# Pixel additions leave GpSimd's queue as their products are done, and SyncE branches ahead of its last wait

## The chip, the core and the metric

The kernel runs on one core of one Trainium2 chip. Its time is device microseconds (us) of one execution on that core; three executions give the median and the spread. Five engines work side by side and meet only at semaphores: TensorE (PE, with its weight loads as PEld), VectorE (DVE), ScalarE (ACT), GpSimd (POOL) and SyncE (SP), which here only issues transfers. Each engine takes its instructions strictly in the order in which they stand in its queue.

## The reference

The input x is 8 images of 24 channels and 64x64 pixels, float32. Two residual stages are computed, both with a normalisation over the 24 channels of a pixel:

```python
x = x + _L0_conv_ref(_ln_c(x))
t = _to_tokens(x)
t = t + _L0_ffn_ref(_ln_t(t), L0_ffn_W1, L0_ffn_b1, L0_ffn_W2, L0_ffn_b2)
x = _from_tokens(t, x)
```

`_L0_conv_ref` multiplies its input by V / (V + 1e-6), a share per pixel that depends on how uneven the channel mean of the normalised input is. That mean is zero but for rounding, so the map is flat and the share is a constant table, unless a check made at run time says otherwise. `_L0_ffn_ref` is a two-layer network (24 to 96, bias, relu, 96 to 24, bias) on values rounded to 8-bit floats (5 exponent bits, 2 mantissa bits), with sums rounded to 16-bit floats.

## The kernel before

The 32768 pixels stand as 8 groups (n = 0 to 7) of 128 partitions x 32 pixels, each with 24 channels: 128x768 float32, 384 KB. For statistics the groups are taken in four units of 1, 1, 2 and 4 groups (u = 0 to 3). Everything stays in on-chip memory between the 9 loads at the start and the 9 stores.

For one group the steps are, with the function that issues each:

- VectorE `centre(n)` (L806): pixels minus the channel mean. The means come from `reduce_pixels` for groups 0 and 1, and else from sums made on TensorE, which `take_sums` copies (L797, L795).
- ScalarE `square(n)`, TensorE `sum_squares(n)` (L607), VectorE `take_var(u)` (L813), ScalarE `first_std(u)`, VectorE `inverse_std(u)` and `conv_gain(s, u)` (three short instructions): the factor by which a centred pixel is multiplied in the first stage.
- the product centred x gain into `result`: `conv(s, n)`, on GpSimd (L372) for groups 0, 1, 2, 4, 5, 6 and on VectorE (L844) for groups 3 and 7.
- `add_pixels(s, n)` (L360): a transfer issued by GpSimd that adds the loaded pixels to `result` in memory.
- ScalarE `second_std`, VectorE `second_inverse`, `second_norm`, and `quantise(s, n)` (L863): the second normalisation, rounded to 8 bits. TensorE `turn(s, n)` (L625) turns it, ScalarE `copy_turned` (L447) copies it.
- the network's first layer in three tiles t = 0, 1, 2: TensorE `first_layer(s, n, t)` (L640), ScalarE `round_hidden(s, n, t)` (L456), VectorE `bias_relu(s, n, t)` (L875), then `quantise_hidden` (L884) for tiles 0 and 1 together and for tile 2.
- the second layer: TensorE `second_layer(s, n)` (L662), ScalarE `round_ffn` (L466), VectorE `second_bias` (L892).
- the last addition: for groups 0 to 4 `add_ffn_by_dma(s, n)` (L366), again a transfer issued by GpSimd; for groups 5 to 7 `add_ffn` on VectorE (L903). Then `store(s, n)` (L327) on SyncE; the last half of group 7 is stored by ScalarE (L473).

`unevenness()`, `find_peak()` and `flag()` make the run-time check; every engine loads its flag (L290) and branches over a second, general pass that is not run on this input. `keep_busy(s, n)` (L675) is three matmuls on zeros whose result nobody reads.

Nothing schedules this work at run time or build time: the order in each queue is written out by hand, as the list of calls in a function `first_groups` of each engine. In the GpSimd list a few waits stand that no data needs, such as `pool.wait_ge(s.hidden_act, 9)`: they set the moment at which a product begins. Waits that data does need stand inside the functions.

## Time and profile before

| what | value |
|---|---|
| three executions | 67.58, 67.95 and 67.13 us, median 67.58 |
| profiled execution | 67.71 us, of which the traced span is 65.8 us |
| VectorE busy | 54.9 us, 83% of the span |
| TensorE busy | 52.0 us, 79% |
| ScalarE busy | 44.1 us, 67% |
| GpSimd busy | 23.9 us, 36% |
| transfers | 12.07 MB in 4475 packets |

The profile comes from one execution. "Busy" counts compute instructions; on GpSimd the issue of an adding transfer is counted too. A duration includes the end of an instruction that overlaps the start of the next one on the same engine, so what an instruction costs its queue is the distance between two starts. Start times are microseconds from the start of the span; the 1.9 us between 67.71 and the span lie outside the trace.

### The profile page before, as it was taken

The page shows a single profiled execution, that of the slowest core. Times are in us where ns is not written, and L with a number is a line of the kernel's source. Part 1 is how long each engine was busy: PE and PEld are TensorE (multiplying, and loading weights), DVE is VectorE, ACT ScalarE, POOL GpSimd, SP SyncE. Part 2 cuts the span into 40 slices and gives each one's busy share as a digit, 9 for nine tenths or more (in the row PEclk, how much of TensorE's full clock was granted, in tenths as well). Part 3 has the DMA queues.
Part 4 walks back from the last instruction along what each step waited for, and adds up shares of the span by engine and source line. Part 5 has one row for each costly group of instructions (what it writes and reads, how often), then busy time and mean ns, then how long its engine had stood idle before and what let it go on. Part 6 is the DMA issues. An engine that isn't in the chain of part 4 may idle for free.

```text
span 65.8 us, 1346 instructions
## 1 busy us (share of the span) xinstructions
PE 52.0 (79%) x471; PEld 36.5 (55%) x475; DVE 54.9 (83%) x113; ACT 44.1 (67%) x67; POOL 23.9 (36%) x25
## 2 busy tenths in 40 slices
PE   2999999999999999959759978979996988460000
PEld 0334999999998999826128335518262627150000
DVE  2059957899799999799999999999999999999300
ACT  5304352287749999279999999999999994450000
POOL 2000001964830000389387989962350580000000
PEclk9999999999999999999999999999999999999655
DMA  0999999009339000001995996999999399999651
GB/s 0 240 420 350 407 405 393 17 10 181 58 60 179 0 0 0 0 0 33 198 187 103 202 228 132 187 312 233 263 286 218 73 304 291 274 284 342 251 177 36
DMA packets 4475, 12.07 MB, mean 183 GB/s; under 512 B 496, under 2 KB 752, under 8 KB 4464
## 3 DMA queue, kind: packets, MB, share of 16 engines
q0 software_dynamic: 1872, 5.11, 39.1%
q1 hardware_dynamic: 2448, 6.62, 27.0%
q10 hardware_dynamic: 144, 0.20, 0.9%
q8 instruction: 6, 0.10, 0.8%
q14 instruction: 5, 0.04, 0.2%
HBM read 3.67 MB, written 3.15 MB: 104 GB/s over the span
## 4 chain that ended last, share of the span: by engine, by line
PE 49%; DVE 16%; ACT 13%; issue 12%; DVEq 2%; ACTq 0%
PE ps_ffn L607 12%; ACT hidden_rounded L456 10%; PE ps_ffn L589 8%; PE ps_ffn L764 8%; PE ps_hidden L640 6%; DVE hidden_q L884 5%; PE ps_ffn L662 5%; PE ps_ffn L579 4%; PE ps_hidden L607 4%; DVE ffn_out L892 3%; DVE hidden_act L875 2%; ACT packed_t L447 2%; DVE result L903 2%; DVE packed L863 1%; PE ps_turned L625 1%
## 5 line engine op out<-in xcount | busy, mean ns | idle before, releaser
L456 ACT ACTIVATE hidden_rounded<-ps_hidden 128x1024 f16<-128x1024 f32 x24 | 23.8, 1031 | 0.0
L372 POOL TENSOR_TENSOR result<-centred,gain 128x768 f32<-128x768 f32 x6 | 11.2, 1866 | 21.4 <-DVE scaled_var L837 10.4
L640 PE MATMUL ps_hidden<-packed_t,w1q 96*128 96x512 fp8e5 x48 | 14.0, 380 | 1.5 <-ACT packed_t L447 0.8
L875 DVE TENSOR_SCALAR hidden_act<-hidden_rounded,b1q 128x1024 f16<-128x1024 f16 x24 | 11.5, 478 | 0.0
L425 ACT ACTIVATE squares<-centred 128x768 f32<-128x768 f32 (+1 forms) x9 | 6.8, 769 | 4.6 <-DVE centred L806 4.6
L662 PEld LDWEIGHTS ps_ffn<-w2q,hidden_q 128*128 128x128 fp8e5 x168 | 7.6, 98 | 2.9 <-DVE hidden_q L884 2.4
L360 POOL DMA_DIRECT2D result<-loaded x8 | 8.4, 1103 | 1.8 <-POOL result L372 1.5
L662 PE MATMUL ps_ffn<-w2q,hidden_q 128*128 128x96 fp8e5 x168 | 8.3, 206 | 0.7 <-DVE hidden_q L884 0.7
L884 DVE TENSOR_SCALAR hidden_q<-hidden_act 128x2048 uint16<-128x2048 uint16 (+1 forms) x16 | 8.8, 549 | 0.1
L607 PEld LDWEIGHTS ps_ffn<-squares,loaded 128*128 128x128 f32 x72 | 8.6, 192 | 0.4
L607 PE MATMUL ps_ffn<-squares,loaded 128*128 128x128 f32 x72 | 8.7, 275 | 0.0
L806 DVE SCALAR_TENSOR_TENSOR centred<-ps_values,loaded 128x768 f32<-128x768 f32 (+1 forms) x9 | 7.5, 863 | 0.1
L863 DVE TENSOR_TENSOR packed<-centred,ps_values 128x768 fp8e5<-128x768 f32 x8 | 7.4, 946 | 0.0
L366 POOL DMA_DIRECT2D result<-ffn_out x5 | 4.6, 919 | 6.4 <-DVE ffn_out L892 5.9
L640 PEld LDWEIGHTS ps_hidden<-packed_t,w1q 96*128 96x128 fp8e5 x48 | 3.5, 98 | 5.4 <-ACT hidden_rounded L456 2.3
L466 ACT ACTIVATE ffn_rounded<-ps_ffn 128x768 f16<-128x768 f32 x7 | 5.7, 816 | 1.1 <-DVE ffn_out L892 1.0
L764 PE MATMUL ps_ffn<-warm 128*128 128x512 bf16 x12 | 5.3, 629 | 1.2 <-DVE warm L1175 1.2
L589 PE MATMUL ps_ffn<-loaded 128*128 128x128 f32 x48 | 5.7, 276 | 0.0
L589 PEld LDWEIGHTS ps_ffn<-loaded 128*128 128x128 f32 x48 | 5.5, 192 | 0.0
L786 DVE TENSOR_REDUCE ps_values<-loaded 128x32 f32<-128x768 f32 x2 | 3.0, 1482 | 2.8 <-DMA loaded<-in_load 2.8
L447 ACT ACTIVATE packed_t<-ps_turned 96x512 bf16<-96x512 bf16 x8 | 4.8, 599 | 0.5 <-PE ps_turned L625 0.4
L892 DVE TENSOR_TENSOR ffn_out<-ffn_rounded,b2q 128x768 f16<-128x768 f16 (+1 forms) x9 | 5.0, 562 | 0.0
(54 smaller groups left out, 54.5 us busy)
## 6 DMA issues: line engine op xcount, KB each, us to landing
result<-loaded POOLq DMA_DIRECT2D x8, 384.0 KB, 4.6
out<-result SPq DMA_DIRECT2D x7, 384.0 KB, 3.5
loaded<-in_load SPq DMA_DIRECT2D x6, 384.0 KB, 6.1
result<-ffn_out POOLq DMA_DIRECT2D x5, 384.0 KB, 5.2
loaded<-in_load SPq DMA_DIRECT2D x2, 448.0 KB, 4.1
loaded<-in_load SPq DMA_DIRECT2D x1, 385.5 KB, 7.8
out<-result SPq DMA_DIRECT2D x1, 192.0 KB, 2.5
out<-result ACTq DMA_DIRECT2D x1, 192.0 KB, 4.0
```

The source lines that it names most:

```text
L360: pool.dma_start(result[:, n], pixels[n], accum_op=ALU.add).then_inc(s.residual[n], 16)
L372: nc.gpsimd.tensor_tensor(result[:, n], centred[:, n], group_values(gain, n), ALU.mult).then_inc(s.conv_pool, 1)
L456: nc.scalar.activation(hidden_rounded[:, i % HIDDEN_BUFS], ps_hidden[:, i % 2], ACT.Copy).then_inc(s.hidden_rounded, 1)
L589: last = nc.tensor.matmul(ps_late_channels, ident, late_pixels[:, :, c, :], start=(c == 0), stop=(c == C - 1))
L607: last = nc.tensor.matmul(ps_square[u][:, n - UNIT_START[u]], ident, squares[:, n, c * GPIX:(c + CB) * GPIX], start=(c == 0), stop=(c == C ...
L640: last = nc.tensor.matmul(ps_hidden[:, i % 2, b * BANK:(b + 1) * BANK], w1q[:, t * P:(t + 1) * P], packed_t[:, n % 2].bitcast(E5M2)[:, b:: ...
L662: last = nc.tensor.matmul(ffn_banks(n)[:, half, at * CQ:(at + 1) * CQ], hidden_q[:, n % 2, t, col * P:(col + 1) * P].bitcast(E5M2)[:, 0::2 ...
L764: nc.tensor.matmul(ps_ffn[:, i % 2], warm[:, 0:P], warm[:], start=True, stop=True)
L806: nc.vector.scalar_tensor_tensor(centred[:, n, lo:hi, :], group_values(channel_sums, n)[:, lo:hi, :], -1.0 / C, pixels[n][:, lo:hi, :], AL ...
L863: nc.vector.tensor_tensor(packed[:, n % 2].rearrange("p j (c q) b -> p j c b q", q=Q), centred[:, n].rearrange("p c (j b q) -> p j c b q", ...
L875: nc.vector.tensor_scalar(hidden_act[:, n % 2, t], hidden_rounded[:, (n * TILES + t) % HIDDEN_BUFS], b1q[:, t:t + 1], 0.0, ALU.add, ALU.ma ...
L884: nc.vector.tensor_scalar(hidden_q[:, n % 2, lo:hi], hidden_act[:, n % 2, lo:hi].bitcast(U16), 1.0 / 256, None, ALU.mult).then_inc(s.hidde ...
```

## The change

No instruction is added or dropped, but for one jump on SyncE. On GpSimd each pixel addition now follows the product it needs: group 3's addition comes ahead of group 2's product, group 7's ahead of the second transfers of groups 1 to 4, and the first product waits for a later event. The waits that set when products begin are others. On SyncE group 3 is stored ahead of group 2, and the wait for all stores stands behind the branch. On VectorE, ScalarE and TensorE the lists of calls are put in another order.

```diff
@@ SyncE
                 store(s, 0)
                 store(s, 1)
+                store(s, 3)
                 store(s, 2)
-                store(s, 3)
                 store(s, 4)
...
             uneven_map = is_uneven(sp)
-
-            sp.wait_ge(flat_pass.stored, 16 * (NG + 1))
             with sp.If(uneven_map):
+
+                sp.wait_ge(flat_pass.stored, 16 * (NG + 1))
...
+            sp.wait_ge(flat_pass.stored, 16 * (NG + 1))
@@ GpSimd
-                pool.wait_ge(s.scaled_var, 1)
+                pool.wait_ge(s.norm2, 2)
                 conv(s, 0)
                 add_pixels(s, 0)
-                pool.wait_ge(s.norm2, 2)
+                pool.wait_ge(centred_vector, 6)
                 conv(s, 1)
                 add_pixels(s, 1)
-                pool.wait_ge(s.hidden_act, 4)
+                add_pixels(s, 3)
+                pool.wait_ge(s.hidden_q, 2)
                 conv(s, 2)
                 add_pixels(s, 2)
-                add_pixels(s, 3)
-                pool.wait_ge(s.hidden_act, 6)
+                add_ffn_by_dma(s, 0)
+                pool.wait_ge(s.hidden_act, 5)
                 conv(s, 4)
                 add_pixels(s, 4)
-                add_ffn_by_dma(s, 0)
-                pool.wait_ge(s.hidden_act, 9)
+                pool.wait_ge(s.norm2, 4)
                 conv(s, 5)
                 add_pixels(s, 5)
+                add_pixels(s, 7)
                 add_ffn_by_dma(s, 1)
-                pool.wait_ge(s.hidden_act, 11)
+                pool.wait_ge(s.hidden_act, 12)
                 conv(s, 6)
...
                 add_ffn_by_dma(s, 4)
-                add_pixels(s, 7)
@@ TensorE
-                second_layer(s, 1)
@@ VectorE
+                conv(s, 7)
...
-                conv(s, 7)
```

How the queues stand now, first GpSimd's, from group 2's product on. Before (L372 is a product, L360 a pixel addition, L366 the addition of the network's output; the wait in brackets tells the group of the last two kinds):

```order
L372 TENSOR_TENSOR result<-centred,gain 128x768 [waits centred_vector,gain0,hidden_act0]
L360 DMA result<-loaded 128x768 [waits conv_pool0]
L360 DMA result<-loaded 128x768 [waits conv_vector0]
L372 TENSOR_TENSOR result<-centred,gain 128x768 [waits centred_vector,gain0,hidden_act0]
L360 DMA result<-loaded 128x768 [waits conv_pool0]
L366 DMA result<-ffn_out 128x768 [waits ffn_out0,residual0_0]
L372 TENSOR_TENSOR result<-centred,gain 128x768 [waits centred_vector,gain0,hidden_act0]
L360 DMA result<-loaded 128x768 [waits conv_pool0]
L366 DMA result<-ffn_out 128x768 [waits ffn_out0,residual0_1]
```

And in the changed kernel, from group 3's pixel addition on (every line number is one higher):

```order
L361 DMA result<-loaded 128x768 [waits conv_vector0]
L373 TENSOR_TENSOR result<-centred,gain 128x768 [waits centred_vector,gain0,hidden_q0]
L361 DMA result<-loaded 128x768 [waits conv_pool0]
L367 DMA result<-ffn_out 128x768 [waits ffn_out0,residual0_0]
L373 TENSOR_TENSOR result<-centred,gain 128x768 [waits centred_vector,gain0,hidden_act0]
L361 DMA result<-loaded 128x768 [waits conv_pool0]
L373 TENSOR_TENSOR result<-centred,gain 128x768 [waits centred_vector,gain0,norm2_0]
L361 DMA result<-loaded 128x768 [waits conv_pool0]
L361 DMA result<-loaded 128x768 [waits conv_vector0]
L367 DMA result<-ffn_out 128x768 [waits ffn_out0,residual0_1]
```

Group 5's product now waits for `second_norm` of the last unit and no longer stands behind group 0's second transfer; both additions that wait for VectorE's products (conv_vector0) have moved ahead.

The second place is VectorE, from the second `second_inverse` of the last unit to the middle of group 2's hidden tiles. Before:

```order
L849 RECIPROCAL inv_std<-std 128x128
L875 TENSOR_SCALAR hidden_act<-hidden_rounded,b1q 128x1024
L884 TENSOR_SCALAR hidden_q<-hidden_act 128x1024
L892 TENSOR_TENSOR ffn_out<-ffn_rounded,b2q 128x8x24x4
L875 TENSOR_SCALAR hidden_act<-hidden_rounded,b1q 128x1024
L854 SCALAR_TENSOR_TENSOR ps_values<-gain,inv_std 128x128
L875 TENSOR_SCALAR hidden_act<-hidden_rounded,b1q 128x1024
L863 TENSOR_TENSOR packed<-centred,ps_values 128x96x2x4 x2
L892 TENSOR_TENSOR ffn_out<-ffn_rounded,b2q 128x8x24x4
```

Now:

```order
L850 RECIPROCAL inv_std<-std 128x128
L876 TENSOR_SCALAR hidden_act<-hidden_rounded,b1q 128x1024
L885 TENSOR_SCALAR hidden_q<-hidden_act 128x2048
L855 SCALAR_TENSOR_TENSOR ps_values<-gain,inv_std 128x128
L864 TENSOR_TENSOR packed<-centred,ps_values 128x96x2x4 x2
L876 TENSOR_SCALAR hidden_act<-hidden_rounded,b1q 128x1024
L885 TENSOR_SCALAR hidden_q<-hidden_act 128x1024
L876 TENSOR_SCALAR hidden_act<-hidden_rounded,b1q 128x1024
L845 TENSOR_TENSOR result<-centred,gain 128x768
```

The two `quantise` calls (L863, now L864) come sooner behind `second_norm`, `second_bias` of group 0 has gone to an earlier place and that of group 1 to a later one, and group 7's product stands here in place of 10 us further on.

The third place is TensorE, from `keep_busy(s, 1)` on. Before:

```order
L675 MATMUL ps_ffn<-warm 128x512 x3
L625 MATMUL ps_turned<-ident_bf,packed 96x128 x4
L640 MATMUL ps_hidden<-packed_t,w1q 128x512 x4
L662 MATMUL ps_ffn<-w2q,hidden_q 128x96 x24
L640 MATMUL ps_hidden<-packed_t,w1q 128x512 x4
```

Now:

```order
L676 MATMUL ps_ffn<-warm 128x512 x3
L641 MATMUL ps_hidden<-packed_t,w1q 128x512 x4
L626 MATMUL ps_turned<-ident_bf,packed 96x128 x4
L641 MATMUL ps_hidden<-packed_t,w1q 128x512 x6
L626 MATMUL ps_turned<-ident_bf,packed 96x128 x4
L641 MATMUL ps_hidden<-packed_t,w1q 128x512 x2
L626 MATMUL ps_turned<-ident_bf,packed 96x128 x4
L663 MATMUL ps_ffn<-w2q,hidden_q 128x96 x24
```

Group 1's second layer (x24) has moved behind two more tiles of the first layer and two more turns.

## Rows read from the trace of the kernel before

**Rows 1.** The page: busy us; DMA in 40 slices; the second layer (24 matmuls a group).

```profile
PE 52.0 (79%) x471; PEld 36.5 (55%) x475; DVE 54.9 (83%) x113; ACT 44.1 (67%) x67; POOL 23.9 (36%) x25
...
DMA  0999999009339000001995996999999399999651
...
L662 PE MATMUL ps_ffn<-w2q,hidden_q 128*128 128x96 fp8e5 x168 | 8.3, 206 | 0.7 <-DVE hidden_q L884 0.7
```

**Rows 2.** Timeline of VectorE: start us, us, what, xcount, [idle before <-releaser].

```profile
27.72 0.69 DVE L813 TENSOR_REDUCE square_sums<-ps_ffn 128x128 f32<-128x512 f32 x1 [0.44 <-PE ps_ffn L607]
...
33.98 0.54 DVE L875 TENSOR_SCALAR hidden_act<-hidden_rounded,b1q 128x1024 f16<-128x1024 f16 x1
...
34.78 0.55 DVE L892 TENSOR_TENSOR ffn_out<-ffn_rounded,b2q 128x768 f16<-128x768 f16 x1
35.25 0.48 DVE L875 TENSOR_SCALAR hidden_act<-hidden_rounded,b1q 128x1024 f16<-128x1024 f16 x1
35.64 0.29 DVE L854 SCALAR_TENSOR_TENSOR ps_values<-gain,inv_std 128x128 f32<-128x128 f32 x1
...
36.24 1.81 DVE L863 TENSOR_TENSOR packed<-centred,ps_values 128x768 fp8e5<-128x768 f32 x2
37.97 1.04 DVE L892 TENSOR_TENSOR ffn_out<-ffn_rounded,b2q 128x768 f16<-128x768 f16 x1
...
42.38 0.58 DVE L875 TENSOR_SCALAR hidden_act<-hidden_rounded,b1q 128x1024 f16<-128x1024 f16 x1
```

**Rows 3.** Timeline of GpSimd: three of its six products.

```profile
32.43 1.80 POOL L372 TENSOR_TENSOR result<-centred,gain 128x768 f32<-128x768 f32 x1 [1.01 <-DVE hidden_act L875]
...
36.46 2.13 POOL L372 TENSOR_TENSOR result<-centred,gain 128x768 f32<-128x768 f32 x1
...
40.82 1.85 POOL L372 TENSOR_TENSOR result<-centred,gain 128x768 f32<-128x768 f32 x1
```

**Rows 4.** Timeline of ScalarE.

```profile
28.45 0.40 ACT L432 ACTIVATE std<-square_sums,eps_c 128x128 f32<-128x128 f32 x1 [1.76 <-DVE square_sums L813]
...
31.19 0.81 ACT L466 ACTIVATE ffn_rounded<-ps_ffn 128x768 f16<-128x768 f32 x1
...
32.17 1.93 ACT L456 ACTIVATE hidden_rounded<-ps_hidden 128x1024 f16<-128x1024 f32 x2
33.98 0.61 ACT L447 ACTIVATE packed_t<-ps_turned 96x512 bf16<-96x512 bf16 x1
34.46 1.96 ACT L456 ACTIVATE hidden_rounded<-ps_hidden 128x1024 f16<-128x1024 f32 x2
...
53.08 1.94 ACT L456 ACTIVATE hidden_rounded<-ps_hidden 128x1024 f16<-128x1024 f32 x2
```

**Rows 5.** Timeline of VectorE, the end.

```profile
56.45 0.48 DVE L875 TENSOR_SCALAR hidden_act<-hidden_rounded,b1q 128x1024 f16<-128x1024 f16 x1
...
60.43 1.03 DVE L903 TENSOR_TENSOR result<-result,ffn_out 128x384 f32<-128x384 f32 x2
```

**Rows 6.** Timeline of TensorE: the last sums of squares.

```profile
24.84 2.84 PE L607 MATMUL ps_ffn<-squares,loaded 128*128 128x128 f32 x24
```

**Rows 7.** Stretches: busy us (instructions) of PE, PEld, DVE, ACT, POOL; granted PE clock; DMA share; GB/s.

```profile
32.60:34.60 2.00, 1.13 (x8) 0.36 (x6) 2.00 (x4) 2.00 (x4) 1.70 (x2) 1.00 1.04 189
...
38.00:50.00 12.00, 10.45 (x110) 5.74 (x110) 12.00 (x25) 12.00 (x17) 7.24 (x7) 1.00 0.97 232
...
62.00:65.80 3.80, 0.00 (x0) 0.00 (x0) 0.00 (x0) 0.00 (x0) 0.00 (x0) 0.50 0.38 130
```

**Rows 8.** By line: the stores' landings (L327, then L473), SyncE's branch, VectorE's last instruction.

```profile
DMA to landing us min/median/max: 2.4/3.4/5.1
...
DMA to landing us min/median/max: 4.0/4.0/4.0
...
L345 SPq COMPARE_BRANCH  x1: 45/45/45, 65.5 to 65.5; - x1
...
L151 DVEq DRAIN  x1: 62/62/62, 64.8 to 64.8; - x1
```

More of the change, by code:

```diff
@@ L512, in first_groups @@
                 first_std(2)
+                square(6)
+                copy_turned(s, 1)
                 round_hidden(s, 0, 1)
[L514 to L515 removed]
                 second_std(s, 2)
+                square(7)
                 round_hidden(s, 0, 2)
[L518 removed]
+                first_std(3)
                 round_hidden(s, 1, 0)
[L520 removed]
+                round_ffn(s, 0)
                 round_hidden(s, 1, 1)
@@ L523, in first_groups @@
                 round_hidden(s, 1, 2)
-                round_ffn(s, 0)
                 second_std(s, 3)
@@ L721, in first_groups @@
                 second_layer(s, 0)
+                first_layer(s, 1, 1)
+                first_layer(s, 1, 2)
+                turn(s, 2)
+                keep_busy(s, 1)
                 first_layer(s, 2, 0)
                 first_layer(s, 2, 1)
-                keep_busy(s, 1)
                 turn(s, 3)
@@ L1079, in first_groups @@
                 centre(1)
+                take_sums(0)
+                centre(2)
                 take_var(0)
+                centre(3)
                 inverse_std(0)
+                take_var(1)
                 conv_gain(s, 0)
-                take_sums(0)
+                inverse_std(1)
+                conv_gain(s, 1)
                 second_inverse(s, 0)
-                take_var(1)
-                centre(2)
-                inverse_std(1)
                 second_norm(s, 0)
-                conv_gain(s, 1)
                 quantise(s, 0)
@@ L1092, in first_groups @@
                 second_norm(s, 1)
-                centre(3)
                 quantise(s, 1)
@@ L1108, in first_groups @@
                 bias_relu(s, 0, 2)
+                second_norm(s, 2)
                 quantise_hidden(s, 0, 2, 3)
-                second_norm(s, 2)
-                bias_relu(s, 1, 0)
                 take_var(3)
@@ L1114, in first_groups @@
                 inverse_std(3)
+                bias_relu(s, 1, 0)
+                second_bias(s, 0)
+                conv_gain(s, 3)
                 bias_relu(s, 1, 1)
-                conv_gain(s, 3)
-                quantise_hidden(s, 1, 0, 2)
-                bias_relu(s, 1, 2)
                 quantise(s, 3)
                 second_inverse(s, 3)
+                bias_relu(s, 1, 2)
+                quantise_hidden(s, 1, 0, 2)
+                second_norm(s, 3)
+                quantise(s, 4)
+                quantise(s, 5)
                 bias_relu(s, 2, 0)
                 quantise_hidden(s, 1, 2, 3)
-                second_bias(s, 0)
                 bias_relu(s, 2, 1)
-                second_norm(s, 3)
+                conv(s, 7)
                 bias_relu(s, 2, 2)
-                quantise(s, 4)
-                quantise(s, 5)
-                second_bias(s, 1)
                 quantise_hidden(s, 2, 0, 2)
                 bias_relu(s, 3, 0)
+                second_bias(s, 1)
+                bias_relu(s, 3, 1)
                 quantise_hidden(s, 2, 2, 3)
-                bias_relu(s, 3, 1)
+                bias_relu(s, 3, 2)
                 quantise(s, 6)
                 quantise(s, 7)
-                bias_relu(s, 3, 2)
+                bias_relu(s, 4, 0)
                 quantise_hidden(s, 3, 0, 2)
-                bias_relu(s, 4, 0)
+                bias_relu(s, 4, 1)
                 quantise_hidden(s, 3, 2, 3)
-                bias_relu(s, 4, 1)
                 second_bias(s, 2)
@@ L1147, in first_groups @@
                 second_bias(s, 3)
+                unevenness()
                 quantise_hidden(s, 5, 0, 2)
                 bias_relu(s, 5, 2)
-                conv(s, 7)
+                second_bias(s, 4)
+                quantise_hidden(s, 5, 2, 3)
                 bias_relu(s, 6, 0)
-                quantise_hidden(s, 5, 2, 3)
                 bias_relu(s, 6, 1)
-                second_bias(s, 4)
-                unevenness()
+                flag()
                 bias_relu(s, 6, 2)
@@ L1159, in first_groups @@
                 quantise_hidden(s, 6, 2, 3)
-                flag()
+                second_bias(s, 5)
                 bias_relu(s, 7, 1)
-                second_bias(s, 5)
                 quantise_hidden(s, 7, 0, 2)
```

63 lines of the change are left out of this document (28 added, 35 removed).

## The prediction

> **What bounds the kernel now.** I read the page first [rows 1]: VectorE is the busiest engine at 54.9 us, and TensorE's 52.0 us hold three-matmul fillers that nobody waits for. The DMA row has a hole between 22 and 30 us and stands at 9 almost without a break from 31 to 61 us. Then the timelines. From 17.7 us to its last addition at 61.46 us [rows 5] VectorE has one wait of any size, 0.44 us at 27.72 [rows 2], for the last sums of squares. ScalarE waits 1.76 us for the same event [rows 4] and is busy for all of the 12 us from 38 to 50 [rows 7]. So in the middle both queues are full, and the question for any order is which of them is late at the end. In the profile it is VectorE: ScalarE has rounded its last hidden tile at 55.02 (53.08 + 1.94) [rows 4], VectorE takes it at 56.45 [rows 5]. That is a slack of 1.43 us for ScalarE. Behind 56.45 the end is fixed work: additions up to 61.46, the last store 4.0 us to landing, the branch on SyncE at 65.5, the end at 65.8 [rows 5, 8].
>
> Since no compute instruction is added or dropped, the sum of VectorE's steps stays. The time can move only by what VectorE loses between them: stalls behind GpSimd, waits for others, and the tail.
>
> **Steps used below**, each a distance between two starts: a bias step 0.39 to 0.40 (35.25 to 35.64), a `quantise` 0.87 (36.24 to 37.97 for two) [rows 2]; on ScalarE a hidden tile 0.91 (32.17 to 33.98 for two), a turned copy 0.48 (33.98 to 34.46), `round_ffn` 0.7 (its 0.81 less the 0.1 by which such instructions overlap) [rows 4].
>
> **Stalls behind GpSimd's products.** Three VectorE instructions are longer than their like: the bias step at 33.98 has 0.54 instead of 0.48, `second_bias` at 37.97 has 1.04 instead of 0.55, the bias step at 42.38 has 0.58 instead of 0.48 [rows 2]: 0.06 + 0.49 + 0.10 = 0.65 us. Each began while a product ran, and ended 0.3 to 0.4 us after it: the products end at 34.23, 38.59 and 42.67 [rows 3]; the VectorE instructions at 34.52, 39.01 and 42.96. `quantise` beside a product keeps its 0.9 us [rows 2]. So a product costs what pokes out beyond the pair of `quantise` calls that it is put under. Before, group 5's product stands behind group 0's second transfer in GpSimd's queue, begins 0.2 us late and pokes out over a `second_bias`. Now its wait is `second_norm` of the last unit, whose next instructions are two `quantise`: product 1.81 plus some 0.1 of signalling against 2 x 0.87, so it reaches 0.1 to 0.2 into the bias step behind it. Group 6's now waits for the bias step just ahead of two `quantise`, as it did before in effect: 0.10. Group 4's begins ahead of `quantise` and `second_inverse`, as before: 0.06. Sum now 0.10 + 0.10 + 0.06 = 0.26, so **-0.39 us**. Bounds: -0.65 if none pokes out, 0 if the 0.49 comes back at another instruction. Groups 0, 1 and 2 now run under `quantise`, `centre` and `take_var`, which no row shows slowed: 0. Group 7's product on VectorE changes place, not cost.
>
> **The last sums of squares.** On TensorE `first_layer(1, 0)` moves behind them, so they end 0.43 us sooner than 27.68 (24.84 + 2.84) [rows 6], and VectorE's `take_var` starts at 27.28 instead of 27.72. But the bias step that before filled the gap ahead of it (0.40) now comes after: **-0.04 us**. ScalarE had that hidden tile done before its 1.76 us of waiting; now it has 0.91 more to do behind it and the start is 0.44 earlier, so it runs about 0.4 us later than before from here on, which eats into its slack of 1.43.
>
> **New waits of VectorE.** I walked the new order through with the steps above. From 27.28: `take_var` 0.6 (its 0.69 less the overlap [rows 2]), `quantise` 0.87, `inverse_std` as much, bias 0.40, and `second_bias(0)` could begin at 30.01. Its input: TensorE's second layer begins when the variance is taken (28.02) and takes 1.2 (24 of 168 matmuls with 8.3 us, [rows 1]); `round_ffn` begins at 29.3 and ends at 30.1, so a wait of 0.06. `second_inverse(3)` meets its input within 0.02. In the middle VectorE carries group 7's product (0.87) ahead of group 1's `second_bias`, and ScalarE stays ahead. At 47.65 `second_bias(3)` waits for `round_ffn(3)`, whose chain ends near 47.8: 0.17. Near the end the run-time check (1.7 us) now stands ahead of `quantise_hidden` of group 5, so `round_ffn(5)` waits about 0.7 us on ScalarE and the last hidden tile is ready near 55.8 instead of 55.02; VectorE needs it near 56.2. That holds, with 0.4 to 0.5 us left of 1.43. Sum **+0.25 us**; bounds 0 and +1.2 (each of the three double, and the last tile 0.7 late).
>
> **Branch and stores.** SyncE's branch takes 45 ns at 65.5, its engine ends 0.1 later [rows 8]. Now the branch runs while the last store is under way, but a jump stands behind the wait: **-0.05 us**, bounds -0.1 and 0 for this part alone. The pixel addition of group 7, before issued at 52 us into full DMA engines, goes out near 39 us, that of group 3 near 24 us into the hole. No compute instruction waits for either. Group 3's store ahead of group 2's makes the latter wait for a landing near 53.5 us, but five more stores follow anyway. Left is the last store: 4.0 us to landing, where the fastest of the other eight took 2.4 [rows 8]. With less queued it could land earlier, but not for more than 0.7 us of gain, because VectorE's own last instruction stands at 64.8 [rows 8]. Value taken **0**, since the stores of the last three groups and their spacing stay; bounds -0.7 and +0.5.
>
> **Sum.** -0.39 - 0.04 + 0.25 - 0.05 = -0.23 us. Against the profiled execution 67.71 that is 67.48; this one lies 0.13 above the median of 67.58, so the forecast is **67.35 us**.
>
> **Rivals.**
>
> *The tail gets shorter too.* For it: the last store's 4.0 us against 2.4, and 0.9 to 1.0 of DMA share up to 61 us [rows 1, 8], of which one adding transfer of 384 KB is taken away. Against it: stores of groups 2 and 3 move later. Price: the 0.7 above, 66.65 us. Chance 0.25.
>
> *TensorE's clock falls (slower).* Between `keep_busy(1)` and the second layer of group 1, some 31 to 37.7 us, TensorE now has only six first-layer tiles and three turns, each behind a ScalarE step, with gaps up to 0.85 us. The granted clock held 1.00 over 1.13 us of work in 2.00 and shows 0.50, the lower level of 1.2 GHz, after nothing was run [rows 7]. Decides: whether the new light stretch is lighter than the one that held. At the lower level 10.45 us of work in 12.00 [rows 7] is 20.9; if 4 us of that stretch run so, the delay is 4 x (2 x 0.87 - 1) = 3.0, less the slack of 1.43: +1.5 us, 68.85. Chance 0.1.
>
> *VectorE starves.* The waits at +1.2 instead of +0.25, with the stalls saved: 68.3 us. For it: ScalarE keeps less than 0.5 of its slack. Chance 0.1.
>
> *The branch doesn't save but costs.* On VectorE the branch is done near 61.6 and the next instruction stands at 64.8 [rows 8], 3.2 us later. If SyncE's new jump behind the last wait did likewise, the end would come 1 to 3.2 us later, 68.4 to 70.5. Against it: SyncE's queue is short, and its branch before let it go on within 0.1 us [rows 8]. The Trainium skill (Runtime: NRT & Kernel Launch, Instruction fetch mechanics) says that a taken branch whose target isn't in the current two-page window must first fetch the page. By that page VectorE's 3.2 us is such a fetch, which this trace agrees with, and SyncE's jump costs nothing if its few instructions share the window; the time would be 67.35 in one case and 68.4 or more in the other. Chance 0.05.
>
> **How the numbers follow.** The forecast's own case has 0.5. A measurement here tells about 1% from no change (the three runs spread over 0.8 us): below 66.90 is faster, above 68.26 slower. Faster: the tail's 0.25 and a fifth of the forecast's case, 0.35. Slower: 0.1 + 0.05 + 0.05 of the starved case's 0.1, 0.2. Same: 0.45. The range takes in the tail rival with the full -0.65 of the stalls (66.65 - 0.26, 66.4) and reaches up to the starved case and the short end of the dear branch, 68.5.
>
> **What the profile after would show.** Right: no `second_bias` above 0.6 us between 30 and 45 us; `take_var` of the last unit near 27.3; ScalarE's last hidden tile within 0.5 us of VectorE's use; VectorE's last addition ending near 61.2; granted clock 1.00 up to the last matmul. Wrong: idle rows of VectorE that name ScalarE and add up to over 0.5 us, a DRAIN of SyncE well after the last landing, or a last store that lands in under 3 or over 4.5 us; the last alone moves the time by more than all my terms.

## The result and the profile after

| | before | after |
|---|---|---|
| executions, us | 67.58, 67.95, 67.13, 67.20 | 69.30, 69.43, 70.17, 69.38 |
| median, us | 67.39 | 69.41 |
| profiled execution, us (span) | 67.71 (65.8) | 69.30 (67.4) |

The changed kernel is slower: ratio 1.034, 95% interval 1.028 to 1.041. The forecast was 67.35 us with a range up to 68.5. Ratios here and below leave out executions that took over 1.5% longer than the fastest of the same kernel, and so can differ from the quotient of the medians.

The page of the changed kernel, beside [rows 1]: busy us, then the granted TensorE clock and the DMA share in 40 slices of 1.7 us.

```profile
PE 53.9 (80%) x471; PEld 37.6 (56%) x475; DVE 55.1 (82%) x113; ACT 44.2 (66%) x67; POOL 23.3 (35%) x25
...
PEclk9999999999999999999985556999999999999555
DMA  0899999000029481908675999955799819986570
```

VectorE does the same work, 55.1 us against 54.9. What stands out is the clock row: four slices of 5 and 6 in the middle of the work. The profile dates them: the granted clock was 0.50, the lower level of 1.2 GHz, from 34.9 to 41.7 us. Before, it held 1.00 until TensorE had run out of work. The DMA row has thinned from 44 us on, and the time has not followed. In stretches (columns as in [rows 7]) the new order looks so:

```profile
32.00:34.00 2.00, 1.60 (x8) 0.50 (x8) 2.00 (x4) 2.00 (x4) 2.00 (x2) 1.00 0.75 156
34.00:36.00 2.00, 1.03 (x5) 0.25 (x4) 1.97 (x5) 2.00 (x4) 1.67 (x3) 0.72 0.46 106
36.00:38.00 2.00, 2.00 (x9) 0.91 (x8) 2.00 (x4) 1.47 (x2) 1.70 (x2) 0.50 0.93 275
38.00:40.00 2.00, 2.00 (x17) 1.29 (x16) 2.00 (x5) 2.00 (x3) 0.92 (x2) 0.50 1.00 182
40.00:42.00 2.00, 2.00 (x20) 1.49 (x18) 1.00 (x2) 1.09 (x2) 0.75 (x1) 0.57 0.96 174
```

From 36 us TensorE is busy without a gap at the lower clock, and in the last stretch VectorE is idle for half of the time (1.00 of 2.00). The timeline of TensorE names the work (start us, us, what, idle before):

```profile
34.20 0.60 PE L641 MATMUL ps_hidden<-packed_t,w1q 96*128 96x512 fp8e5 x2 [0.18 <-ACT hidden_rounded L457]
...
35.59 1.95 PE L641 MATMUL ps_hidden<-packed_t,w1q 96*128 96x512 fp8e5 x4 [0.79 <-ACT packed_t L448]
...
37.76 1.06 PE L641 MATMUL ps_hidden<-packed_t,w1q 96*128 96x512 fp8e5 x2
...
39.16 2.13 PE L663 MATMUL ps_ffn<-w2q,hidden_q 128*128 128x96 fp8e5 x24
...
43.59 1.19 PE L663 MATMUL ps_ffn<-w2q,hidden_q 128*128 128x96 fp8e5 x24
```

Two first-layer matmuls took 0.60 us at 34.20 and 1.06 at 37.76. Group 1's second layer took 2.13 us, and the same 24 matmuls for the next group, with the clock at 1.00 again, 1.19. The delay is passed on to ScalarE's `round_ffn` and from there to VectorE. ScalarE first, then VectorE:

```profile
41.33 0.81 ACT L467 ACTIVATE ffn_rounded<-ps_ffn 128x768 f16<-128x768 f32 x1 [0.91 <-PE ps_ffn L663]
```

```profile
27.67 0.69 DVE L814 TENSOR_REDUCE square_sums<-ps_ffn 128x128 f32<-128x512 f32 x1 [0.58 <-PE ps_ffn L608]
...
30.75 0.56 DVE L893 TENSOR_TENSOR ffn_out<-ffn_rounded,b2q 128x768 f16<-128x768 f16 x1 [0.35 <-ACT ffn_rounded L467]
...
42.24 0.56 DVE L893 TENSOR_TENSOR ffn_out<-ffn_rounded,b2q 128x768 f16<-128x768 f16 x1 [1.24 <-ACT ffn_rounded L467]
...
45.57 0.75 DVE L876 TENSOR_SCALAR hidden_act<-hidden_rounded,b1q 128x1024 f16<-128x1024 f16 x1
...
62.66 1.03 DVE L904 TENSOR_TENSOR result<-result,ffn_out 128x384 f32<-128x384 f32 x2
```

At 42.24 `second_bias(1)` comes after 1.24 us of idleness, nearly three times the largest wait before [rows 2]. The stalled `second_bias` at 37.97 of [rows 2] is gone, but a bias step at 45.57 now has 0.75 instead of 0.48. GpSimd says why:

```profile
43.34 0.85 POOL L367 DMA_DIRECT2D result<-ffn_out  x1 [2.59 <-DVE ffn_out L893]
44.06 1.97 POOL L373 TENSOR_TENSOR result<-centred,gain 128x768 f32<-128x768 f32 x1
```

Group 1's second transfer stands ahead of group 6's product in the queue, and waited 2.59 us for the late `second_bias(1)`. The product started behind it, at 44.06, and ended at 46.03, 0.29 us before the bias step did. This loss isn't the clock's: with the clock at 1.00, in `after_fill_again` below, the transfer waits 1.25 us and the bias step behind the product still has 0.75.

The span is 1.6 us longer. Cut at VectorE's copy of the last unit's channel sums (17.73 us before, 17.98 after), its last `take_var` and the end of its last addition, that is:

| part | before | after | difference |
|---|---|---|---|
| start, to the copy of the sums | 17.73 | 17.98 | +0.25 |
| copy to `take_var` (27.72, 27.67) | 9.99 | 9.69 | -0.30 |
| `take_var` to VectorE's last addition (61.46, 63.69) | 33.74 | 36.02 | +2.28 |
| tail | 4.34 | 3.71 | -0.63 |

The start's +0.25 goes with a late load: TensorE waited 1.30 us for one in this execution and had no such wait in the one before. In the third part I compared the distances from each VectorE start to the next, step by step: `second_bias(1)` +1.33; the bias step that now follows the variance +0.40; `second_bias(0)` +0.35 (0.35 idle); `second_norm` +0.12; a `quantise_hidden` that uses the bias step directly ahead of it +0.12; stalls beside GpSimd's work 0.53 instead of 0.65, so -0.12. These make 2.20 of the 2.28.

### The profile page after: what moved, and what is told of

Same layout as the page of the kernel before. It is cut to its first block, busy times and chain, and to the rows that moved or that the text cites. A ratio compares the mean times of both kernels' runs of the same rounds, so it can differ in the third digit from the quotient of the medians.

```text
span 67.4 us, 1347 instructions
## 1 busy us (share of the span) xinstructions
PE 53.9 (80%) x471; PEld 37.6 (56%) x475; DVE 55.1 (82%) x113; ACT 44.2 (66%) x67; POOL 23.3 (35%) x25
## 4 chain that ended last, share of the span: by engine, by line
PE 47%; DVE 20%; issue 8%; ACT 8%; DMA 7%; DVEq 2%; SPq 1%; ACTq 0%
PE ps_ffn L608 12%; PE ps_ffn L663 8%; PE ps_ffn L590 8%; DMA loaded<-in_load 7%; PE ps_hidden L641 7%; DVE hidden_act L876 5%; ACT ffn_rounded L467 4%; PE ps_ffn L580 4%; PE ps_hidden L608 4%; DVE ffn_out L893 4%; DVE hidden_q L885 3%; DVE packed L864 2%; ACT hidden_rounded L457 2%; PE ps_turned L626 2%; DVE result L904 2%
## 5 line engine op out<-in xcount | busy, mean ns | idle before, releaser
L641 PE MATMUL ps_hidden<-packed_t,w1q 96*128 96x512 fp8e5 x48 | 15.4, 418 | 2.0 <-ACT packed_t L448 1.3
L663 PEld LDWEIGHTS ps_ffn<-w2q,hidden_q 128*128 128x128 fp8e5 x168 | 8.4, 104 | 3.4 <-DVE hidden_q L885 2.1
L663 PE MATMUL ps_ffn<-w2q,hidden_q 128*128 128x96 fp8e5 x168 | 9.3, 217 | 0.9 <-DVE square_sums L814 0.6
L361 POOL DMA_DIRECT2D result<-loaded x8 | 7.6, 956 | 5.4 <-DVE result L845 3.6
L864 DVE TENSOR_TENSOR packed<-centred,ps_values 128x768 fp8e5<-128x768 f32 x8 | 7.4, 948 | 0.1
L893 DVE TENSOR_TENSOR ffn_out<-ffn_rounded,b2q 128x768 f16<-128x768 f16 (+1 forms) x9 | 4.5, 509 | 1.6 <-ACT ffn_rounded L467 1.6
L765 PE MATMUL ps_ffn<-warm 128*128 128x512 bf16 x12 | 4.2, 520 | 1.2 <-DVE warm L1176 1.2
```

Of the source, the lines that this page charges most:

```text
L361: pool.dma_start(result[:, n], pixels[n], accum_op=ALU.add).then_inc(s.residual[n], 16)
L641: last = nc.tensor.matmul(ps_hidden[:, i % 2, b * BANK:(b + 1) * BANK], w1q[:, t * P:(t + 1) * P], packed_t[:, n % 2].bitcast(E5M2)[:, b:: ...
L663: last = nc.tensor.matmul(ffn_banks(n)[:, half, at * CQ:(at + 1) * CQ], hidden_q[:, n % 2, t, col * P:(col + 1) * P].bitcast(E5M2)[:, 0::2 ...
L864: nc.vector.tensor_tensor(packed[:, n % 2].rearrange("p j (c q) b -> p j c b q", q=Q), centred[:, n].rearrange("p c (j b q) -> p j c b q", ...
```

## The experiments

Each label begins with the kernel that was edited. Every experiment was timed beside `before` on the same chip, whose median is given with it. "Stretch" is the third part of the table above, `take_var` to the end of the last addition: it holds every edit and neither the loads nor the last store, whose durations differ from execution to execution. Its values are 33.74 us for `before` and 36.02 for `after`.

### Is it the clock? `after_fill`, `after_again`, `after_fill_again`

Nine matmuls on zeros, whose result nobody reads, go between the first-layer tiles of the changed kernel, so that TensorE has work where it waited for ScalarE. `fill(k)` is k matmuls of the kind in `keep_busy`.

```diff
                 keep_busy(s, 1)
+                fill(2)
                 first_layer(s, 2, 0)
+                fill(1)
                 first_layer(s, 2, 1)
                 turn(s, 3)
+                fill(2)
                 first_layer(s, 2, 2)
+                fill(3)
                 first_layer(s, 3, 0)
+                fill(1)
                 first_layer(s, 3, 1)
```

> The changed kernel with nine extra filler matmuls (128x512, results unread) on TensorE between keep_busy(1) and group 1's second layer: 2 before and 1 after first_layer(2,0), 2 after turn(3), 3 after first_layer(2,2), 1 after first_layer(3,0). Clock theory: granted clock 1.00 from the start to the last matmul, VectorE's wait for round_ffn(1) falls from 1.24 us to under 0.4, the time to 67.3 to 67.9 us. Rival, the order itself makes group 1's second layer late: the clock holds but VectorE still waits about 1 us there and the time stays at 68.8 us or more.

Measured: median 69.03 us, above the 67.3 to 67.9 expected, beside a before median of 68.04, ratio 1.017 (1.006 to 1.029). The profiled execution had late loads (TensorE waited 2.39 us for one, and took 70.62 us in all), but its stretch is 34.72, the granted clock is 1.00 throughout the middle and `second_bias(1)` doesn't wait. The interval was wide, so I ran the same kernel again beside an unchanged `after`.

> The changed kernel once more, beside the two with fillers on the same chip. Clock theory: granted clock 0.50 for some 6.8 us from about 35 us, VectorE's wait for round_ffn(1) near 1.2 us, time 2 to 3% above the kernel before. If the fall of the clock was an accident of one execution: this profile shows 1.00 there and a ratio near that of the filled kernel.

> The changed kernel with nine extra fillers ahead of group 1's second layer, once more. Clock theory: 1.00 throughout the middle, 1.0 to 1.5 us faster than the changed kernel on the same chip, so 0.5 to 1.2% above the kernel before. Rival, the order alone: within 0.3 us of the changed kernel.

Measured: `after_again` 69.51 us, ratio 1.027 (1.021 to 1.033), stretch 35.47; `after_fill_again` 67.99, ratio 1.008 (1.002 to 1.014), stretch 34.72; before median 67.58. By the medians the fillers give back 1.52 us; in the two profiled executions the stretch shows 0.75 of it, and the rest lies in the start and the tail. Stretches of `after_again`, then of `after_fill_again`:

```profile
34.80:38.20 3.40, 2.22 (x12) 0.69 (x10) 3.37 (x7) 3.39 (x5) 2.80 (x3) 1.00 0.63 182
38.30:41.70 3.40, 3.31 (x32) 2.77 (x32) 3.03 (x6) 2.63 (x3) 1.70 (x2) 0.50 1.03 186
```

```profile
31.00:35.00 4.00, 3.78 (x20) 1.36 (x19) 3.93 (x9) 4.00 (x7) 2.80 (x3) 1.00 0.91 186
35.00:39.00 4.00, 3.68 (x32) 1.75 (x31) 3.96 (x8) 3.89 (x6) 3.58 (x3) 1.00 0.73 158
```

In this execution of the unchanged kernel the clock was low for 3.4 us instead of 6.8, and the step of `second_bias(1)` was 0.68 too long instead of 1.33. So in these two traces the price follows the length of the slow stretch; both ended at 41.7 us. Of the executions without a trace only the mean granted clock is on record. It is 0.909 to 0.957 in all ten of the changed kernel and 0.952 to 0.983 in the ten with fillers; but the four with 0.909 to 0.913 took 69.30 to 70.17 us and the five with 0.951 to 0.957 took 68.84 to 69.99, so the whole time follows the clock only loosely. Where the clock was low in them isn't known.

Two more rows of `after_fill_again` are needed further down: ScalarE's `round_ffn(1)` and VectorE's `second_bias(1)` with the clock at 1.00.

```profile
39.94 0.82 ACT L467 ACTIVATE ffn_rounded<-ps_ffn 128x768 f16<-128x768 f32 x1
```

```profile
41.00 0.54 DVE L902 TENSOR_TENSOR ffn_out<-ffn_rounded,b2q 128x768 f16<-128x768 f16 x1
```

### Or is it the fillers themselves? `after_fill_late`

As many matmuls on zeros, later in the queue, behind the stretch in question.

```diff
                 keep_busy(s, 2)
+                fill(5)
...
                 keep_busy(s, 3)
+                fill(4)
```

> The control: the same nine extra fillers on TensorE, but behind group 1's second layer (5 after keep_busy(2), 4 after keep_busy(3)), where the clock is back. Clock theory: they come too late, the clock falls near 35 us as in the changed kernel and the time is that of the changed kernel or 0 to 0.6 us more. If fillers help by their mere presence: 1 us or more faster than the changed kernel.

Measured: 69.43 us, ratio 1.021 (1.015 to 1.026), near the unchanged kernel's 1.027 and above the 1.008 with the early fillers. The profiled execution, with 73.48 us the longest of the six, began late, with a first slow stretch from 7.7 to 14.5 us, and everything behind it is shifted by 4 to 4.5 us; its stretch is 36.03. The fall in the middle is there, and so is the wait at `second_bias(1)`:

```profile
42.00:45.00 3.00, 3.00 (x29) 2.45 (x30) 3.00 (x7) 2.44 (x3) 1.62 (x3) 0.50 1.00 189
```

```profile
46.29 0.56 DVE L899 TENSOR_TENSOR ffn_out<-ffn_rounded,b2q 128x768 f16<-128x768 f16 x1 [0.73 <-ACT ffn_rounded L467]
```

What follows: in this kernel work on zeros helped ahead of the fall and not behind it.

### Does less work alone bring the fall? `before_nofill`

```diff
-                keep_busy(s, 1)
...
-                keep_busy(s, 2)
```

> The kernel before without keep_busy(1) and keep_busy(2), six filler matmuls whose results nobody reads; the rest is as before. Clock theory: with less TensorE work between 31 and 39 us the granted clock falls to 0.50 there, ScalarE waits for TensorE, and the time rises by 1 to 2.5 us. Rival: the clock holds 1.00 and the time is within 0.2 us of the kernel before, so light work alone does not do it.

Measured: the four executions lie between 67.48 and 70.50 us (median 69.04), too far apart for a ratio. The profiled one took 67.48, with a stretch of 33.72, and its clock held. From 33 to 37 us, busy us of PE alone, the clock, the DMA share and the GB/s; first `before_nofill`, then `after`:

```profile
33.00:35.00 2.00, 0.86 (x6) 1.00 1.00 181
35.00:37.00 2.00, 1.74 (x28) 1.00 0.70 128
```

```profile
33.00:35.00 2.00, 1.61 (x8) 0.97 0.85 201
35.00:37.00 2.00, 1.41 (x4) 0.50 0.42 147
```

TensorE was busy for 0.86 us of 2.00 and the clock stayed up; in the changed kernel it was busy for 1.61 and the clock fell. It isn't the choice of stretch: from 30.9 to 34.9 us, ahead of its fall, the changed kernel had 2.82 us of work, and `before_nofill` had 2.03 from 31.5 to 35.5 and held. So by the busy share the wrong kernel falls. What `before_nofill` kept and `after` lacks there is the second layer, 24 matmuls in a row.

This stands on one trace. The two long executions of `before_nofill`, 70.08 and 70.50 us, had a mean granted clock of 0.938 and 0.930, against 0.959 and 0.961 in the two short ones; but of the seven executions of `before` beside it two are like them (70.16 us with 0.934, 72.69 with 0.917), and without a trace nothing tells where the clock was low. That less work alone makes a fall more frequent is not excluded.

### Is the second layer's move enough? `before_late2`, `before_late2_fill`

The kernel before, with the second layer of group 1 moved behind two more tiles and a turn, and its followers on ScalarE, VectorE and GpSimd moved with it. The second kernel has the same order and nine fillers in the gap.

```diff
@@ TensorE of before_late2
                 first_layer(s, 3, 0)
-                second_layer(s, 1)
                 first_layer(s, 3, 1)
-                first_layer(s, 3, 2)
                 turn(s, 4)
+                first_layer(s, 3, 2)
+                second_layer(s, 1)
@@ ScalarE: round_ffn(s, 1) behind round_hidden(s, 3, 2)
@@ VectorE: second_bias(s, 1) behind bias_relu(s, 3, 1)
@@ GpSimd: the second transfer of group 0 behind group 5's pixel addition, that of group 1 behind group 6's
@@ TensorE of before_late2_fill, on top
                 first_layer(s, 2, 2)
+                fill(3)
                 first_layer(s, 3, 0)
+                fill(3)
                 first_layer(s, 3, 1)
+                fill(2)
                 turn(s, 4)
                 first_layer(s, 3, 2)
+                fill(1)
                 second_layer(s, 1)
```

> The kernel before (with GpSimd's queue as in before_pool2), with one step moved: group 1's second layer stands behind two more first-layer tiles and turn(4) on TensorE, its round_ffn behind them on ScalarE and its second_bias behind bias_relu(3,1) on VectorE, where by the steps of the trace nobody waits for it. Theory: this move alone makes the granted clock fall to 0.50 near 35 us, with a wait of VectorE or ScalarE behind it, 0.5 to 2 us slower than the kernel before. Rival: the fall needs the rest of the change too (VectorE's and ScalarE's order); then the clock holds 1.00 and the time is within 0.4 us of the kernel before.

> The same with nine extra filler matmuls between first_layer(2,2) and the moved second layer. Theory: the clock holds 1.00 and the time is within 0.4 us of the kernel before. If before_late2 is slow here too at a clock of 1.00, the late second layer itself is the cost.

Measured, before median 68.00: `before_late2` 70.88 us, six executions from 68.73 to 73.58, too far apart for a ratio, and by the medians more than the 0.5 to 2 us expected; the profiled one, the longest, has the stretch at 38.95, and the clock at 0.50 from 37.5 to 47.8 us:

```profile
34.00:37.50 3.50, 2.07 (x10) 0.59 (x10) 3.50 (x9) 3.50 (x6) 2.19 (x3) 1.00 0.84 154
37.50:47.80 10.30, 8.72 (x65) 6.08 (x66) 7.75 (x13) 5.61 (x7) 7.22 (x6) 0.50 0.80 158
```

```profile
42.56 1.11 DVE L892 TENSOR_TENSOR ffn_out<-ffn_rounded,b2q 128x768 f16<-128x768 f16 x1 [1.73 <-ACT ffn_rounded L466]
```

ScalarE, full before from 38 to 50 us [rows 7], is busy for 5.61 us of 10.30. The five executions of 70.25 us and more have a mean granted clock of 0.908 to 0.945. The one of 68.73 us has 0.966, which is where `before` beside it lies (0.959 to 0.981 in ten of eleven executions), so the move brings a long fall in most executions and not in all.

`before_late2_fill`: 69.28 us, ratio 1.026 (1.018 to 1.035), clock 1.00 throughout, stretch 35.67. The fillers took 3.3 us off the stretch, but 1.9 us over `before` stayed, where I had expected at most 0.4. GpSimd and VectorE show them:

```profile
40.60 2.28 POOL L372 TENSOR_TENSOR result<-centred,gain 128x768 f32<-128x768 f32 x1
```

```profile
40.85 2.46 DVE L900 TENSOR_TENSOR ffn_out<-ffn_rounded,b2q 128x768 f16<-128x768 f16 x1 [0.39 <-ACT ffn_rounded L466]
```

In its new place `second_bias(1)` waits 0.39 us for ScalarE, then meets group 6's product, and is held until 0.43 us after its end: 2.46 us for an instruction of 0.55. So the move costs twice, by the clock and by what it then stands beside; only the first is what the changed kernel paid.

### GpSimd's order alone: `before_pool`, `before_pool2`, `after_mended`

`before_pool` takes over the early part of the new GpSimd list and puts both second transfers ahead of group 6's product. `before_pool2` moves only the two transfers, each behind a pixel addition.

```diff
@@ before_pool
-                pool.wait_ge(s.scaled_var, 1)
+                pool.wait_ge(s.norm2, 2)
                 conv(s, 0)
                 add_pixels(s, 0)
-                pool.wait_ge(s.norm2, 2)
+                pool.wait_ge(centred_vector, 6)
                 conv(s, 1)
                 add_pixels(s, 1)
+                add_pixels(s, 3)
...
                 add_pixels(s, 2)
-                add_pixels(s, 3)
@@ before_pool and before_pool2
                 add_pixels(s, 4)
-                add_ffn_by_dma(s, 0)
...
                 add_pixels(s, 5)
+                add_ffn_by_dma(s, 0)
@@ before_pool2 only
-                add_ffn_by_dma(s, 1)
...
                 add_pixels(s, 6)
+                add_ffn_by_dma(s, 1)
```

> The kernel before with GpSimd's queue alone changed, as far as the old VectorE order allows: the later first product, group 3's pixel addition ahead of group 2's product, group 0's second transfer behind group 5's product. If second_bias(1) is stalled by that product: its 1.04 us falls to 0.6 to 0.75, the time by 0.3 us. Rival, the stall is hidden elsewhere: second_bias shortens but the time stays within 0.1 us.

> The kernel before, with group 0's second transfer behind group 5's product and group 1's behind group 6's on GpSimd, nothing else: each product begins as soon as its wait allows. If a product blocks a VectorE instruction that shares its path to memory until it ends: second_bias(1) falls from 1.04 to 0.6 to 0.7 us and the bias step behind the second pair of quantise stays at 0.58, the stretch from take_var(3) to the last addition is 0.3 to 0.4 us shorter, the time 0.3 us. Rival, the later transfers come back at the stores: the stretch shortens but the time does not.

Measured: `before_pool` 69.18 us beside 68.04, ratio 1.022 (1.009 to 1.034), stretch 34.24. VectorE, then GpSimd:

```profile
38.32 0.67 DVE L892 TENSOR_TENSOR ffn_out<-ffn_rounded,b2q 128x768 f16<-128x768 f16 x1
...
42.37 1.45 DVE L875 TENSOR_SCALAR hidden_act<-hidden_rounded,b1q 128x1024 f16<-128x1024 f16 x1
```

```profile
39.71 1.99 POOL L366 DMA_DIRECT2D result<-ffn_out  x2
41.00 2.54 POOL L372 TENSOR_TENSOR result<-centred,gain 128x768 f32<-128x768 f32 x1
```

The stall at `second_bias` shrank from 1.04 to 0.67 as hoped. But the issue of the two transfers lasts until 41.70 (39.71 + 1.99). Group 6's product, recorded from 41.00, ends at 43.54 instead of 42.67 [rows 3], and the bias step at 42.37 is held for 1.45 instead of 0.58: 0.37 won, 0.87 lost. The stretch's 0.50 is less than half of the 1.14 between the medians, and what made the rest stays open. `before_pool2` keeps the first (the same 0.67) without the second: 67.74 us beside 67.58, ratio 1.004 (0.999 to 1.009), stretch 33.46, 0.28 less than before. Its ratio doesn't tell it from no change, so the 0.28 stands on one trace.

`after_mended` is `after_fill` with `second_bias(0)`, `second_bias(5)` and group 1's second transfer one place later each, to take the remaining waits away.

```diff
-                second_bias(s, 0)
                 conv_gain(s, 3)
+                second_bias(s, 0)
...
-                second_bias(s, 5)
                 bias_relu(s, 7, 1)
+                second_bias(s, 5)
...
-                add_ffn_by_dma(s, 1)
...
                 add_pixels(s, 6)
+                add_ffn_by_dma(s, 1)
```

> The changed kernel with the nine fillers and three more edits: second_bias(0) behind conv_gain(3), second_bias(5) behind bias_relu(7,1), and group 1's second transfer behind group 6's product. By the ledger of VectorE's steps these give back 0.35, 0.12 and 0.17 us: 34.1 us from take_var(3) to the last addition instead of 34.7, and 0.4 to 0.7 us less time than the filled kernel, equal to the kernel before within 0.4 us. Rival: what is given back there is lost again at a later wait.

Measured: 68.89 us beside 68.00, ratio 1.010 (0.997 to 1.023), stretch 35.07, which is 0.35 worse than without the mending. GpSimd, then VectorE:

```profile
33.53 2.14 POOL L373 TENSOR_TENSOR result<-centred,gain 128x768 f32<-128x768 f32 x1
```

```profile
34.81 1.15 DVE L885 TENSOR_SCALAR hidden_act<-hidden_rounded,b1q 128x1024 f16<-128x1024 f16 x1
```

Each edit did what it was made for: beside `after_fill_again`, VectorE's steps are 0.43, 0.22 and 0.10 us shorter at the three places. Each gain was lost elsewhere. Group 0's second transfer, issued at 32.96, had to wait for `second_bias(0)` in its later place, so group 4's product slid under a bias step, which ended 0.29 us after it and had 1.15 us: 0.56 lost. `second_inverse` now waits for ScalarE (0.34), and a step near the end is 0.29 longer.

### Branch and tail: `before_branch`, `before_early7`

```diff
@@ before_branch, SyncE
-            sp.wait_ge(flat_pass.stored, 16 * (NG + 1))
             with sp.If(uneven_map):
+                sp.wait_ge(flat_pass.stored, 16 * (NG + 1))
...
+            sp.wait_ge(flat_pass.stored, 16 * (NG + 1))
@@ before_early7: before_pool2, and on VectorE and GpSimd
                 quantise_hidden(s, 2, 0, 2)
+                conv(s, 7)
...
-                conv(s, 7)
...
                 add_pixels(s, 6)
+                add_pixels(s, 7)
...
-                add_pixels(s, 7)
```

> The kernel before with SyncE's change alone: the wait for all stores behind the branch, none of the reordering. If the branch change is worth only what the branch took: within 0.1 us of the kernel before. If the new jump has to fetch its target after the last landing: 1 us or more slower.

> The kernel before_pool2 with group 7's product moved on VectorE from behind bias_relu(5,2) to behind quantise_hidden(2,0,2), and its pixel addition ahead of group 1's second transfer: the change's own idea at the place that its title names, without the other reordering. If an adding transfer of 384 KB less in the last 14 us empties the DMA engines: the last store lands in 3.0 to 3.4 us instead of 3.8 to 4.0 and the time falls by 0.4 to 0.7 us against the kernel before, with the 0.3 of before_pool2 on top. Rival: the last landing varies by itself and the time stays where before_pool2 has it.

Measured: `before_branch` 67.84 us beside 68.04, in 66.76 to 68.15, too few and too far apart for a ratio. By line its end reads:

```profile
L151 SPq COMPARE_BRANCH  x1: 38/38/38, 65.3 to 65.3; - x1
...
L151 SPq DRAIN  x1: 7/7/7, 65.4 to 65.4; - x1
```

The branch that stood behind the wait has gone ahead of it, and in its place stands a jump of 38 ns instead of 45, with the engine's last instruction 0.1 us on. The trace shows neither a gain of 0.05 us nor a loss of 1 us; the time can't tell the first from nothing. VectorE's own last instruction stands at 65.5 here, behind SyncE's, so an earlier end of SyncE would hardly have been felt.

`before_early7` had 69.75 us beside 68.00, ratio 1.019 (1.002 to 1.037), with a stretch of 34.02 in the profiled execution. The half of group 7 that ScalarE stores landed in 3.3 us instead of 4.0, but a store of SyncE, issued at 62.9 us, was the last to land and the end came no sooner: SyncE's branch stands at 67.1. VectorE's steps from 49.08 to 51.29 came to 0.58 us more than in `before_pool2`, the last of them a wait of 0.23 for ScalarE's `round_ffn`. Taking group 7's pixel addition out of the busy time gained nothing that I could show. ScalarE's store, over `before` and all my variants of it, landed in 2.9 to 4.0 us, without an order in it that follows the edits.

## Why the prediction was wrong

**The step that failed is the clock: the sum has no term for it, and "TensorE's clock falls" got a chance of 0.1.** The runs showed the granted clock at 0.50 for 6.8 and 3.4 us, from 34.9 and 38.3 on; +1.33 us at `second_bias(1)` in the profiled pair; and 1.52 between the medians with and without fillers. The rival named the place (31 to 37.7 us) and a price of +1.5. It is shown from both sides: fillers ahead of the fall take the loss away, fillers behind it don't, and the second layer's move, with what follows it on the other engines, puts the fall into the kernel before, in most executions.

That the price came so near is luck, since neither part of it holds. It was a delay of 3.0 us less a slack of 1.43. `round_ffn(1)` ended at 42.14 us in the changed kernel and at 40.76 in `after_fill_again`, where the clock held, so the delay was 1.4 us. And the 1.43 us were ScalarE's slack at the last hidden tile; here `second_bias(1)` began at 41.00, so the slack was 0.24.

What misled me was the test that I wrote beside it, whether the new light stretch is lighter than the 1.13 us in 2.00 that had held [rows 7]. I compared busy time. `before_nofill` shows 0.86 of 2.00 that held. The third listing of the order, in the section on the change, shows what the busy time hides: before, 4 + 4 matmuls of the first layer with 24 of the second between them; after, nothing but first-layer tiles and turns, each at ScalarE's pace. A block of 24 matmuls that no engine interrupts was what I moved, and it should have set the weight of the rival at even chances or more. That it is this block which the clock answers to fits all traces here, but was tried in one kernel only, and never with the block at a third place. Of the signs that I had listed, no `second_bias` above 0.6 us came true, because the loss had moved in front of the instruction; the clock and VectorE's idle rows that name ScalarE (1.24 + 0.35 us) said wrong.

**Without the fall** the kernel is still no faster: ratio 1.008 (1.002 to 1.014). By the forecast's own terms:

- *Stalls behind products*, forecast -0.39: -0.12 in the profiled pair. Groups 4 and 5 came about as forecast (0.09 and 0 for 0.06 and 0.10). Group 6's product "now waits for the bias step just ahead of two `quantise`", I wrote; in fact it waited in its queue behind group 1's second transfer, whose input came later. Its 0.27 in place of 0.10 is the largest part; the rest are three steps longer by 0.06 to 0.07. I had listed the transfer in the order and not put its wait into the product's start.
- *The last sums of squares*, forecast -0.04: the variance started 0.30 sooner after the sums instead of 0.44, and with the 0.40 behind it the term is +0.10.
- *New waits of VectorE*, forecast +0.25: beside the clock's 1.33 there are 0.35 at `second_bias(0)`, which I had at 0.06, and 0.12 + 0.12, so +0.59. The first comes from ScalarE and TensorE: the second layer of group 0 began 0.26 us after the variance was taken (28.62 against 28.36), not with it. The wait that I expected at `second_bias(3)`, 0.17, did not come, and not only because VectorE was late: in `after_fill_again`, with the clock at 1.00, it starts at 48.92, 0.40 behind the bias step before it, as without a wait. The last hidden tile came as forecast: there ScalarE is done with it at 56.96 and VectorE takes it at 57.42, 0.46 us later.
- *Branch*, forecast -0.05: about 0, by the trace of `before_branch`. The rival in which it costs 1 us or more fell with it: SyncE goes on within 0.1 us in both kernels. The 3.2 us between VectorE's branch and its last instruction [rows 8] have no like on SyncE, so a fetch such as the Trainium skill (Runtime: NRT & Kernel Launch, Instruction fetch mechanics) ties to a taken branch doesn't show on the queue that was edited.
- *Tail*, forecast 0 with -0.7 as its lower end: -0.63, since the last store landed in 3.3 us instead of 4.0. The range held it. It can't be put down to the change, since variants of `before` landed in 2.9 to 4.0.
- *Start*, not in the forecast: +0.25, with a late load; `after_fill` and `after_fill_late` had later ones.

The terms of the order, -0.12 + 0.10 + 0.59 + 0 = +0.57 us, are 0.8% of the time, which is what the ratio without the fall says, within its wide interval. So the direction would have been wrong without the clock as well, by a small amount: of the 0.39 us to be gained at the stalls 0.12 came, and I had too few small waits.

**One mechanism held in every trace.** A bias step or `second_bias` that meets a product on GpSimd ends 0.28 to 0.43 us after that product, however early it began: 0.67, 0.75, 1.15, 1.45 and 2.46 us in the rows above, for instructions of 0.5. (A `quantise_hidden` that met one, in both kernels with the late second layer, had 0.80 instead of 0.68.) So what counts isn't a slower rate but the whole time from its own start to the product's end, and an order that moves an engine by 0.3 us can lose 1 us to it. The Trainium skill (SBUF — State Buffer, SBUF: two separate sides) calls the port pair that VectorE shares with GpSimd an exclusive lock: whoever starts first has it for the whole instruction, the other "fully blocks". It limits this to VectorE instructions in a two-port mode or with two inputs in on-chip SBUF; `quantise`, one of whose inputs lies in PSUM, kept 0.9 us beside a product [rows 2, 3]. The rows agree with the blocking and with its limit. They show it one way only: in each the product was recorded first, and none shows GpSimd held up by VectorE.

## What to carry to other kernels

Before moving a long block of matmuls on an engine that else runs at another engine's pace, look at what it leaves behind, not at the busy share: if only short pieces remain that each wait for someone, take a fall of the granted clock as likely (by this one kernel), and price it at the place where it would be felt, with the slack of that place. If the order is wanted all the same, put fillers into the gap ahead of the fall. And of a product on GpSimd, work out its start from the transfers queued ahead of it, their inputs and the time of their issue (0.85 to 1.3 us each in these traces), then see which VectorE instruction its end meets: taking a wait away moves it too.

## What was unexpected of the hardware

The slow stretch wasn't of one length: 6.8 and 3.4 us in two executions of the changed kernel, 10.3 us in `before_late2`, beginning at 34.9, 38.3 and 37.5 us, the step's excess 1.33 and 0.68 us in the first two. What ends or lengthens it no run here tells; nor was it tried how much of the second layer would have had to stay.

Products on GpSimd are recorded with 2.54, 2.28 and 2.14 us in the rows above and 2.13 before [rows 3], against 1.80 to 1.82 where no transfer's issue stands just ahead. They look slower, and they are the ones that hold up VectorE longest. But each of them is recorded from a moment at which the issue ahead of it hasn't ended. The issues ahead, in `before` and in `after_mended`:

```profile
35.88 0.86 POOL L366 DMA_DIRECT2D result<-ffn_out  x1 [0.47 <-issue]
```

```profile
32.96 0.86 POOL L367 DMA_DIRECT2D result<-ffn_out  x1 [2.15 <-DVE ffn_out L902]
```

From the end of the issue (36.74, 33.82, 41.70 in `before_pool`, 41.04 in `before_late2_fill`) to the end of the product it is 1.85, 1.85, 1.84 and 1.84 us. So the extra length is the overlap of the two records, and it is the transfer ahead that moves the product's end, and with it the end of the VectorE instruction.
